# The Vector engine's order at the step boundary of a Runge-Kutta loop: a seed between two transposes, and FFN work ahead of the cubic term

## The chip, the cores and the metric

The kernel runs on one NeuronCore of a Trainium2 chip. The metric is the time of one execution on the device in microseconds (us). Engines are named as in the profile: PE (matmul), PEld (its weight load), DVE (Vector), ACT (Scalar), POOL (GpSimd), SP (the queue that issues most DMAs). L1313 is line 1313 of the kernel.

## The reference

```
x = x + attn(gru(cond, x))                    # 64 sequential GRU steps, then attention
x = x + ffn(rk4(cond, cond, drive=x))         # 64 sequential RK4 steps, FFN on their results

def _derivative(q, p, drive, coupling, bias):
    i_couple = jnp.tanh(q) @ coupling.T
    dq = q - q ** 3 / 3.0 - p + drive + i_couple + bias
    dp = EPSILON * (q + ALPHA - BETA * p)

dq1, dp1 = _derivative(q, p, drive, coupling, bias)
dq2, dp2 = _derivative(q + 0.5 * DT * dq1, p + 0.5 * DT * dp1, drive, coupling, bias)
dq3, dp3 = _derivative(q + 0.5 * DT * dq2, p + 0.5 * DT * dp2, drive, coupling, bias)
dq4, dp4 = _derivative(q + DT * dq3, p + DT * dp3, drive, coupling, bias)
q_next = clip(q + DT / 6.0 * (dq1 + 2 * dq2 + 2 * dq3 + dq4), -CLAMP, CLAMP)
```

The state q is 32 x 512. Four derivatives, each with a tanh and a product with a 512 x 512 matrix, follow one another in each of 64 steps. The FFN (gate, up, down, with its operands rounded to fp8) has 2048 rows, four steps' worth making a tile of 128 rows.

## The kernel before, in words

The program has three parts: the GRU, the attention, and from about 1009 us on the Runge-Kutta steps with the FFN woven in. Only the third is touched.

**Stages.** A step has four stages (st 0 to 3), stage number n = 4t + st. Four steps form a group g of 16 stages, counted k = 0 to 15. After each stage comes a "slot", a piece of the FFN for tiles made from earlier groups. The order on each engine is written out by hand: DVE, ACT, PE and POOL each run `stage` and `slot` in turn. Groups 0 to 2 and 15 are written out; groups 3 to 14 are a hardware loop of twelve passes. Groups 0 and most of 1 have no FFN work yet.

**One stage.** DVE turns the state in two halves (L1271, `state_turned`), ACT takes the tanh of each half (L961), PE multiplies with the coupling matrix in 32 matmuls (L750) into a PSUM bank that already holds a "seed", and DVE combines the bank with a cubic term `ebuf` (L1313). Then the next stage's halves are turned. The seed is written by DVE: for st 1 to 3 at L1292, right after the cubic term of the stage before; for st 0 at L1290, at the boundary between two steps. PE's L750 of a stage waits for its seed (rk_seed) and for the tanh of its first half, and from its 17th matmul on for the second half. After the 32 matmuls PE runs `mix_into` (L740), which waits for the seed of the next stage and has 1, 2 or 3 products in the stages 0, 1 and 2, and then the PE part of the slot (gate/up products L764, down products L811, transposes L775 and L785).

**The cubic term.** ACT squares the state into PSUM (L953), DVE makes `ebuf` from it (L1304). In st 1 to 3 ACT squares before the tanhs. In st 0 it squares after them, and it needs the clamped state, which DVE writes at L1326 (the boundary's last instruction), so L1304 of st 0 waits for a chain DVE, ACT, DVE.

**The boundary.** At the end of st 3 DVE runs: combination (L1313), both transposes (L1271), the seed of the next step (L1290, which waits for POOL's clamped p, rk_p, L519, and for the drive's sum), the clamp (L1326). Then st 0: cubic term (L1304), seed of st 1 (L1292), the slot's FFN piece, the drive's sum for the following step (L1281), combination (L1313).

**The FFN pieces that stand in st 0.** k = 0 and k = 12: one gate part (L1436, reads PSUM). k = 4: one gated part (L1444, reads PSUM, waits for POOL's L524 of slot 3). k = 8: a copy of one column (L1353) and `t_bits` on 768 columns (L1410, memory to memory), while POOL adds and subtracts the rounding grid of another tile (L538 and L543, 512 columns each, memory to memory).

Of the kernel before, what the change touches and what calls it, by code (L numbers as in the profile page):

```python
# [87 lines left out]
def wait_if(eng, sem, value):  # L88

    if not isinstance(value, int) or value > 0:  # L90
        eng.wait_ge(sem, value)
# [45 lines left out]
def gru_attn_rk4_ffn(nc, xT, x, cond_quad, cond_T, W_ih, W_hh, gate_bias, state_bias, gamma, Wq, Wkv, Wo,  # L137
                     couplingT, bias_quad, w_gate, w_up, w_down, down_idx, ident, mean_of, trig, mask,
                     x1_scr, q_scr, wgu_scr, wd_scr, scale_scr, tok_scr, out):
    with ExitStack() as ctx:  # L140
# [6 lines left out]
        def f32(a, *dims):  # L147
            n = 1
            for d in dims:
                n *= d  # L150
            v = mem[:, a:a + n]
            if len(dims) == 2:
                v = v.rearrange("p (a b) -> p a b", a=dims[0])
            if len(dims) == 3:
                v = v.rearrange("p (a b c) -> p a b c", a=dims[0], b=dims[1])
            return v
# [85 lines left out]
        qsT = f32(w.take(P), NC, B)  # L242
# [784 lines left out]
        def _(dve):  # L1027
# [237 lines left out]
            dve.tensor_scalar(pn[1], pn[1], -ALPHA / BETA, None, ALU.add).then_inc(rk_start, 1)  # L1265
            dve.wait_ge(rk_bits, 1)

            def state_turned(src):

                for half in range(2):  # L1270
                    dve.transpose(qsT[:, 2 * half:2 * half + 2, :].rearrange("p c b -> p (c b)"), src[:, half * 64:half * 64 + 64]).then_inc(rk_qT, 1)  # L1271
            state_turned(qn[3])
            dve.wait_ge(rk_start, 3)

            def driven(s):
                return ps[:, 4, (s % 2) * P:(s % 2 + 1) * P]

            def drive_sum(t, s, loads):

                dve.wait_ge(drive_ld[s], 16 * loads)  # L1280
                dve.tensor_tensor(driven(s), drive[s], bias_ps, ALU.add).then_inc(rk_drive, 1)  # L1281

            def seed(t, s, st):

                p = pn[(s - 1) % 2]
                o = ps[:, st % 2, 0:P]
                if st == 0:
                    dve.wait_ge(rk_drive, t + 1)
                    wait_if(dve, rk_p, t)
                    dve.tensor_tensor(o, driven(s), p, ALU.subtract).then_inc(rk_seed, 1)  # L1290
                else:
                    dve.scalar_tensor_tensor(out=o, in0=p, scalar=float(SEEDS[st][0]), in1=driven(s), op0=ALU.mult, op1=ALU.add).then_inc(rk_seed, 1)  # L1292
# [4 lines left out]
            def stage(g, s, st, last, fill):  # L1297
                t = 4 * g + s
                n = 4 * t + st
                qs = qn[(s - 1) % 4] if st == 0 else qst[st - 1]  # L1300
                stt = dve.scalar_tensor_tensor
                end = last and s == 3
                dve.wait_ge(rk_sq, n + 1)
                stt(out=ebuf, in0=ps[:, 5, 0:P], scalar=KEPT[st], in1=qs, op0=ALU.subtract, op1=ALU.mult).then_inc(rk_e, 1)  # L1304
                if st < 3:
                    seed(t, s, st + 1)
                fill()
                if st == 0 and not (last and s == 3):
                    drive_sum(t + 1, (s + 1) % 4, g + 1 + (s == 3))
                dve.wait_ge(rk_e, n + 1)  # L1310
                dve.wait_ge(rk_mm, n + 1)
                dst = qst[st] if st < 3 else ps[:, 4, 2 * P:3 * P]
                stt(out=dst, in0=ps[:, st % 2, 0:P], scalar=STEP[st], in1=ebuf, op0=ALU.mult,  # L1313
                    op1=ALU.subtract).then_inc(rk_qs if st < 3 else rk_pre, 1)
                if st < 3:
                    dve.wait_ge(rk_qs, n + 1)
                else:
                    dve.wait_ge(rk_pre, t + 1)
                if not (end and st == 3):
                    state_turned(dst)  # L1320
                if st == 3:
                    if not end:
                        seed(t + 1, (s + 1) % 4, 0)

                    wait_if(dve, q_wr[s], PRIMED + 16 * g)
                    dve.tensor_scalar(qn[s], dst, CLAMP, -CLAMP, ALU.min, ALU.max).then_inc(rk_qs, 1)  # L1326

# [121 lines left out]
            def group(g, rk, tile):  # L1449
                if not isinstance(g, int):  # L1450
                    base = counts["lead"] + (g - LEAD) * GROUP_STEPS
                else:
                    base = counts.get("next", 0)
                v = Steps(dve, rk_v, base)
                if isinstance(g, int) and g == 1:
                    dve.wait_ge(ffn_ld, 16 * 6)
                for k in range(16):
                    if rk:
                        stage(g, k // 4, k % 4, isinstance(g, int) and g == NTILE - 1, lambda: slot(v, k, tile, rk))
                    else:  # L1460
                        slot(v, k, tile, rk)
                if isinstance(g, int):
                    counts["next"] = counts.get("next", 0) + v.n
                    if g == LEAD - 1:
                        counts["lead"] = counts["next"]
                else:
                    assert v.n == GROUP_STEPS, v.n
                    counts["next"] += (NTILE - 1 - LEAD) * GROUP_STEPS
# [74 lines left out]
```

## Time and profile before

| | us |
|---|---|
| median of 3 runs | 1643.82 |
| lowest, highest | 1642.74, 1644.45 |
| the profiled execution | 1640.76 |
| its span, first to last instruction | 1638.8 |
| outside the span | 2.0 |
| third part, first combination to last | 1012.2 to 1593.0 |
| PE, DVE, ACT, POOL busy over the span | 91%, 68%, 36%, 23% |

Start times are in us from the span's start. The end of a DVE or ACT instruction is its start plus its length, but the next one can start before that: two records of one engine overlap, and the distance between starts is what an instruction costs in a row of them. Where the idle time before an instruction is given, the engine or line behind the arrow is what ended it.

### The profile page before, as it was taken

Reading aid. Unit: us, or ns where it says so; the run is one execution under the profiler, and the core shown is the slowest. Engines: PE = TensorE matmul, PEld = TensorE weight load, DVE = VectorE, ACT = ScalarE, POOL = GpSimd, SP = SyncE. Lnnn points to the kernel's source line nnn. Section 1 sums busy time; section 2 is a strip of 40 time slices with the busy share of each in tenths; the row PEclk is TensorE's granted clock in tenths of the full one; section 3 lists DMA queues with packets and bytes.
Section 4 is the critical chain, followed back from the end, with each engine's and each line's share of the span. In section 5 each row is a group of like instructions: output and inputs, shape, how many; then the busy total and the mean of one; then the engine's idle time right before and its main releaser. Section 6 shows DMA issues by size and latency. Waiting matters only on the chain.

```text
span 1638.8 us, 46339 instructions
## 1 busy us (share of the span) xinstructions
PE 1489.4 (91%) x16583; PEld 927.8 (57%) x16624; DVE 1119.8 (68%) x3565; ACT 588.7 (36%) x1903; POOL 381.5 (23%) x545
## 2 busy tenths in 40 slices
PE   5999999996799999999999997678899999999984
PEld 1333333334575767667675844556666666666662
DVE  1667667765774747575664732578888888888886
ACT  1444444441102020201102021455555555555552
POOL 0221221210000000000000000245655555556550
PEclk8999999997899999999999998999999999999996
DMA  7111112116101000100000024001111111111111
GB/s 304 44 45 50 51 46 65 51 47 167 9 1 26 0 26 0 26 0 26 6 19 13 13 64 163 21 25 29 40 40 40 33 35 32 35 32 43 37 38 33
DMA packets 91035, 72.79 MB, mean 44 GB/s; under 512 B 32480, under 2 KB 82912, under 8 KB 89824
## 3 DMA queue, kind: packets, MB, share of 16 engines
q1 hardware_dynamic: 71184, 59.35, 12.4%
q10 hardware_dynamic: 18032, 6.88, 1.7%
q0 software_dynamic: 1760, 5.77, 1.2%
q8 instruction: 37, 0.61, 0.2%
q14 instruction: 22, 0.18, 0.0%
HBM read 55.03 MB, written 16.94 MB: 44 GB/s over the span
## 4 chain that ended last, share of the span: by engine, by line
PE 73%; DVE 13%; ACT 5%; issue 5%; DMA 1%; POOL 1%; DVEq 0%; SPq 0%; POOLq 0%; ACTq 0%
PE ps L655 13%; PE ps L645 13%; PE ps L750 11%; PE ps L583 11%; PE ps L595 10%; PE ps L689 3%; PE ps L713 3%; ACT mem L961 3%; DVE mem L1313 2%; DVE mem L1271 2%; PE ps L740 2%; ACT ps L953 2%; PE ps L764 1%; PE ps L666 1%; DVE ps L1281 1%
## 5 line engine op out<-in xcount | busy, mean ns | idle before, releaser
L750 PE MATMUL ps<-mem 128*32 128x128 f32 x8192 | 278.8, 276 | 68.5 <-ACT mem L961 65.8
L750 PEld LDWEIGHTS ps<-mem 128*32 128x32 f32 x8192 | 211.4, 110 | 143.0 <-ACT mem L961 97.2
L645 PE MATMUL ps<-mem 128*128 128x512 f32 x512 | 224.6, 592 | 0.0
L655 PE MATMUL ps<-mem 128*128 128x256 f32 x1024 | 222.3, 379 | 0.0
L655 PEld LDWEIGHTS ps<-mem 128*128 128x128 f32 x1024 | 194.0, 190 | 26.0
L509 POOL TENSOR_TENSOR mem<-mem 128x128 f32<-128x128 f32 x64 | 30.8, 481 | 732.8 <-ACT mem L956 732.8
L583 PE MATMUL ps<-mem 128*32 128x384 f32 x2048 | 181.6, 497 | 10.2 <-DMA mem<-in_W_ih 6.3
L595 PE MATMUL ps<-mem 128*32 128x384 f32 x2048 | 177.6, 488 | 2.4 <-DVE mem L1098 2.4
L928 ACT ACTIVATE mem<-mem 128x512 f32<-128x512 f32 x32 | 19.7, 630 | 391.0 <-DVE mem L1211 391.0
L645 PEld LDWEIGHTS ps<-mem 128*128 128x128 f32 x512 | 95.6, 190 | 109.7 <-issue 109.3
L961 ACT ACTIVATE mem<-mem 128x64 f32<-128x64 f32 x512 | 102.9, 248 | 116.5 <-DVE mem L1271 116.4
L953 ACT ACTIVATE ps<-mem 128x128 f32<-128x128 f32 x256 | 72.0, 281 | 182.2 <-DVE mem L1313 175.8
L740 PE MATMUL ps<-mem 128*128 128x128 f32 x768 | 137.0, 301 | 0.0
L513 POOL TENSOR_TENSOR mem<-mem 128x128 f32<-128x128 f32 x192 | 99.8, 520 | 155.7 <-ACT mem L956 149.6
L595 PEld LDWEIGHTS ps<-mem 128*32 128x32 f32 x2048 | 62.9, 110 | 109.5 <-issue 81.0
L583 PEld LDWEIGHTS ps<-mem 128*32 128x32 f32 x2048 | 64.3, 111 | 105.5 <-issue 90.8
L740 PEld LDWEIGHTS ps<-mem 128*128 128x128 f32 x768 | 100.2, 190 | 38.4 <-issue 25.9
L1174 DVE TENSOR_TENSOR mem<-ps,mem 64x256 f32<-64x256 f32 x272 | 114.7, 422 | 8.5
L1172 DVE TENSOR_TENSOR mem<-ps,mem 128x256 f32<-128x256 f32 x136 | 57.8, 425 | 69.9 <-PE ps L666 40.8
L764 PE MATMUL ps<-mem 128*128 128x352 bf16 x512 | 100.3, 322 | 3.5 <-DVE mem L1436 3.4
L480 POOL COPY mem<-mem 128x128 f32 (+1 forms) x64 | 37.7, 590 | 276.2 <-DVE mem L1098 276.2
L1304 DVE SCALAR_TENSOR_TENSOR mem<-ps,mem 128x128 f32<-128x128 f32 x256 | 74.5, 291 | 22.4 <-ACT ps L953 22.4
(139 smaller groups left out, 2097.0 us busy)
## 6 DMA issues: line engine op xcount, KB each, us to landing
mem<-x_scr SPq DMA_DIRECT2D x128, 64.0 KB, 1.8
mem<-in_xT SPq DMA_DIRECT2D x64, 64.0 KB, 1.9
mem<-in_Wq SPq DMA_DIRECT2D x1, 4096.0 KB, 12.4
mem<-in_Wo SPq DMA_DIRECT2D x1, 4096.0 KB, 20.7
mem<-in_x SPq DMA_DIRECT2D x16, 256.0 KB, 2.8
x_scr<-mem SPq DMA_DIRECT2D x32, 128.0 KB, 2.3
q_scr<-mem SPq DMA_DIRECT2D x64, 64.0 KB, 1.6
mem<-q_scr SPq DMA_DIRECT2D x64, 64.0 KB, 1.9
```

The lines of the kernel that those rows point to most:

```text
L513: tt(pacc, pacc, pw[1 + st], ALU.add).then_inc(rk_pa, 1)
L583: mm = pe.matmul(ps[32 * j:32 * j + 32, par, 0:3 * P].rearrange("p (g n) -> p g n", g=3), xt[par][:, c, :], wih[:, c, :].rearrange("p (g j ...
L595: mm = pe.matmul(ps[32 * j:32 * j + 32, par, P:4 * P].rearrange("p (g n) -> p g n", g=3), hT[1 - par][:, c, :], whh[:, c, :].rearrange("p ...
L645: mm = pe.matmul(ps[:, 6 + pr, :], aoT[:, h, pr * P:pr * P + P], wo[:, h, :], start=(h == 0), stop=(h == HEADS - 1))
L655: mm = pe.matmul(ps[:, h % Q_BANKS, 0:BLK], wq[:, c, h * DH:(h + 1) * DH], xnb[:, c, :], start=(c == 0), stop=(c == NC - 1))
L740: pe.matmul(ps[:, st % 2, 0:P], mix[m], (None, qn[(s - 1) % 4], *qst)[k], start=False, stop=False, skip_group_check=True)
L750: mm = pe.matmul(ps[32 * j:32 * j + 32, st % 2, 0:P], thT[:, c, :], ct[:, c, j * P:(j + 1) * P], start=False, stop=(c == NC - 1), skip_gro ...
L764: mm = pe.matmul(ps[:, 2 + order % 2, 0:GU_N], qxT[:, c, :], (wgT if gate else wuT)[:, c, m * GU_N:(m + 1) * GU_N], start=(c == 0), stop=( ...
L953: act.activation(ps[:, 5, 0:P], src, ACT.Square, scale=(STEP[st] / 3) ** 0.5).then_inc(rk_sq, 1)
L961: act.activation(thT[:, 2 * half:2 * half + 2, :], qsT[:, 2 * half:2 * half + 2, :], ACT.Tanh).then_inc(rk_th, 1)
L1174: dve.tensor_tensor(share[b:b + DH // 2], src[a:a + DH // 2], bcast(trigs[:, tr + 1, :], BLK_B)[a:a + DH // 2], ALU.mult).then_inc(done, 1)
L1304: stt(out=ebuf, in0=ps[:, 5, 0:P], scalar=KEPT[st], in1=qs, op0=ALU.subtract, op1=ALU.mult).then_inc(rk_e, 1)
```

## The change

`state_turned` is split so that each half can be written alone. At the boundary the next step's seed goes between the two transposes. In stage 0 the FFN's piece (`fill`) goes ahead of the cubic term, and the drive's sum stands behind the seed of stage 1. Stages 1 to 3 keep their order.

```diff
+            def turned_half(src, half):
+
+                dve.transpose(qsT[:, 2 * half:2 * half + 2, :].rearrange("p c b -> p (c b)"), src[:, half * 64:half * 64 + 64]).then_inc(rk_qT, 1)
+
...
                 end = last and s == 3
+                if st == 0:
+                    fill()
                 dve.wait_ge(rk_sq, n + 1)
                 stt(out=ebuf, in0=ps[:, 5, 0:P], scalar=KEPT[st], in1=qs, op0=ALU.subtract, op1=ALU.mult).then_inc(rk_e, 1)
                 if st < 3:
                     seed(t, s, st + 1)
-                fill()
-                if st == 0 and not (last and s == 3):
+                if st:
+                    fill()
+                elif not end:
                     drive_sum(t + 1, (s + 1) % 4, g + 1 + (s == 3))
...
-                if not (end and st == 3):
+                if st < 3:
                     state_turned(dst)
-                if st == 3:
+                else:
                     if not end:
+                        turned_half(dst, 0)
                         seed(t + 1, (s + 1) % 4, 0)
-
+                        turned_half(dst, 1)
                     wait_if(dve, q_wr[s], PRIMED + 16 * g)
                     dve.tensor_scalar(qn[s], dst, CLAMP, -CLAMP, ALU.min, ALU.max).then_inc(rk_qs, 1)
```

Only DVE's row changes; the rows of PE, ACT, POOL and SP stay in their order. DVE in the loop, from the boundary into k = 4, before (L1271 the transposes, L1290 the seed of st 0, L1326 the clamp, L1304 the cubic term, L1292 the seed of st 1, L1444 the FFN piece, L1281 the drive's sum, L1313 the combination):

```order
L1271 STREAM_TRANSPOSE mem<-ps 128x64 [waits rk_pre]
L1271 STREAM_TRANSPOSE mem<-ps 128x64
L1288 REGISTER_ALU
L1290 TENSOR_TENSOR ps<-ps,mem 128x128 [waits rk_p,rk_drive]
L91 ISA
L1326 TENSOR_SCALAR mem<-ps 128x128 [waits q_wr0]
L1303 ISA
L1304 SCALAR_TENSOR_TENSOR mem<-ps,mem 128x128 [waits rk_sq]
L1292 SCALAR_TENSOR_TENSOR ps<-mem,ps 128x128
L1444 SCALAR_TENSOR_TENSOR mem<-ps,mem 128x352 [waits f_sgu,f_u]
L1281 TENSOR_TENSOR ps<-mem,ps 128x128 [waits drive_ld2]
L1313 SCALAR_TENSOR_TENSOR mem<-ps,mem 128x128 [waits rk_mm,rk_e]
```

The same place now (the lines are, in that order of names: L1270, L1293, L1333, L1309, L1295, L1451, L1284, L1319):

```order
L1270 STREAM_TRANSPOSE mem<-ps 128x64 [waits rk_pre]
L1291 REGISTER_ALU
L1293 TENSOR_TENSOR ps<-ps,mem 128x128 [waits rk_p,rk_drive]
L1270 STREAM_TRANSPOSE mem<-ps 128x64
L91 ISA
L1333 TENSOR_SCALAR mem<-ps 128x128 [waits q_wr0]
L1451 SCALAR_TENSOR_TENSOR mem<-ps,mem 128x352 [waits f_sgu,f_u]
L1308 ISA
L1309 SCALAR_TENSOR_TENSOR mem<-ps,mem 128x128 [waits rk_sq]
L1295 SCALAR_TENSOR_TENSOR ps<-mem,ps 128x128
L1284 TENSOR_TENSOR ps<-mem,ps 128x128 [waits drive_ld2]
L1319 SCALAR_TENSOR_TENSOR mem<-ps,mem 128x128 [waits rk_mm,rk_e]
```

The seed has changed places with the second transpose, and the FFN piece, with its waits on POOL (f_sgu) and PE (f_u), has moved past the cubic term and the seed of st 1. DVE in the loop, from the boundary into k = 8, before (L1353 the copy of a column, L1410 `t_bits`):

```order
L1290 TENSOR_TENSOR ps<-ps,mem 128x128 [waits rk_p,rk_drive]
L1326 TENSOR_SCALAR mem<-ps 128x128 [waits q_wr1]
L1303 ISA
L1304 SCALAR_TENSOR_TENSOR mem<-ps,mem 128x128 [waits rk_sq]
L1292 SCALAR_TENSOR_TENSOR ps<-mem,ps 128x128
L1353 COPY mem<-mem 128x1 [waits f_gated]
L1409 ISA
L1410 TENSOR_SCALAR mem<-mem 128x768 [waits f_vt]
L1281 TENSOR_TENSOR ps<-mem,ps 128x128 [waits drive_ld3]
```

And now (L1360 the copy, L1417 `t_bits`):

```order
L1293 TENSOR_TENSOR ps<-ps,mem 128x128 [waits rk_p,rk_drive]
L1270 STREAM_TRANSPOSE mem<-ps 128x64
L1333 TENSOR_SCALAR mem<-ps 128x128 [waits q_wr1]
L1360 COPY mem<-mem 128x1 [waits f_gated]
L1416 ISA
L1417 TENSOR_SCALAR mem<-mem 128x768 [waits f_vt]
L1308 ISA
L1309 SCALAR_TENSOR_TENSOR mem<-ps,mem 128x128 [waits rk_sq]
L1295 SCALAR_TENSOR_TENSOR ps<-mem,ps 128x128
L1284 TENSOR_TENSOR ps<-mem,ps 128x128 [waits drive_ld3]
```

Here the piece that moved is a memory-to-memory instruction. PE's row at this place, unchanged, after the 32 matmuls of k = 8:

```order
L738 REGISTER_ALU
L740 MATMUL ps<-mem 128x128 [waits rk_seed]
L811 MATMUL ps<-mem 128x512 [waits f_tTcp]
L811 MATMUL ps<-mem 128x512 x2
L748 ISA [waits rk_seed]
L750 MATMUL ps<-mem 32x128 [waits rk_th]
```

The down products and the next stage's L750 are queued behind L740, which waits for the seed of st 1.

## Rows read from the trace of the kernel before

**Rows 1.** The page: busy time by engine; the chain that ended last.

```profile
PE 1489.4 (91%) x16583; PEld 927.8 (57%) x16624; DVE 1119.8 (68%) x3565; ACT 588.7 (36%) x1903; POOL 381.5 (23%) x545
PE 73%; DVE 13%; ACT 5%; issue 5%; DMA 1%; POOL 1%; DVEq 0%; SPq 0%; POOLq 0%; ACTq 0%
```

**Rows 2.** Timeline, DVE, k = 15 into k = 0: start, length, engine, line, operation.

```profile
1301.46 0.30 DVE L1313 SCALAR_TENSOR_TENSOR ps<-ps,mem 128x128 f32<-128x128 f32 x1 [0.47 <-PE ps L750]
1301.79 0.38 DVE L1271 STREAM_TRANSPOSE mem<-ps 128x64 f32<-128x64 f32 x2
1302.10 0.27 DVE L1290 TENSOR_TENSOR ps<-ps,mem 128x128 f32<-128x128 f32 x1
1302.27 0.27 DVE L1326 TENSOR_SCALAR mem<-ps 128x128 f32<-128x128 f32 x1
1302.90 0.29 DVE L1304 SCALAR_TENSOR_TENSOR mem<-ps,mem 128x128 f32<-128x128 f32 x1 [0.35 <-ACT ps L953]
1303.10 0.28 DVE L1292 SCALAR_TENSOR_TENSOR ps<-mem,ps 128x128 f32<-128x128 f32 x1
1303.30 0.58 DVE L1436 SCALAR_TENSOR_TENSOR mem<-ps,mem 128x352 f32<-128x352 f32 x1
1303.79 0.28 DVE L1281 TENSOR_TENSOR ps<-mem,ps 128x128 f32<-128x128 f32 x1
1303.99 0.28 DVE L1313 SCALAR_TENSOR_TENSOR mem<-ps,mem 128x128 f32<-128x128 f32 x1
```

**Rows 3.** Timeline, ACT, the same boundary and the next stage.

```profile
1302.08 0.40 ACT L961 ACTIVATE mem<-mem 128x64 f32<-128x64 f32 x2 [1.54 <-DVE mem L1271]
...
1304.58 0.40 ACT L961 ACTIVATE mem<-mem 128x64 f32<-128x64 f32 x2
```

**Rows 4.** Timeline, PE: k = 15, 0 and 1; last, k = 9.

```profile
1300.24 1.08 PE L750 MATMUL ps<-mem 128*32 128x128 f32 x32 [0.18 <-ACT mem L961]
...
1302.50 1.08 PE L750 MATMUL ps<-mem 128*32 128x128 f32 x32
1303.51 0.49 PE L740 MATMUL ps<-mem 128*128 128x128 f32 x2
...
1304.89 1.08 PE L750 MATMUL ps<-mem 128*32 128x128 f32 x32 [0.30 <-ACT mem L961]
...
1323.04 1.08 PE L750 MATMUL ps<-mem 128*32 128x128 f32 x32 [0.29 <-ACT mem L961]
```

**Rows 5.** Timeline, ACT and PE, first boundary of group 0, written out, no FFN.

```profile
1020.24 0.40 ACT L961 ACTIVATE mem<-mem 128x64 f32<-128x64 f32 x2 [1.62 <-DVE mem L1271]
...
1020.64 1.08 PE L750 MATMUL ps<-mem 128*32 128x128 f32 x32 [1.15 <-ACT mem L961]
```

**Rows 6.** Timeline, POOL and DVE, k = 3 and 4, the same loop pass.

```profile
1310.78 0.93 POOL L524 TENSOR_TENSOR mem<-mem 128x352 f32<-128x352 f32 x1
...
1313.02 0.28 DVE L1313 SCALAR_TENSOR_TENSOR mem<-ps,mem 128x128 f32<-128x128 f32 x1
```

**Rows 7.** Timeline, POOL, then DVE, boundary into k = 8, the same loop pass.

```profile
1320.07 1.27 POOL L538 TENSOR_TENSOR mem<-mem 128x512 f32<-128x512 f32 x1
1321.50 1.65 POOL L543 TENSOR_TENSOR mem<-mem 128x512 bf16<-128x512 f32 x1 [0.16 <-POOL mem L538]
...
1320.39 0.27 DVE L1326 TENSOR_SCALAR mem<-ps 128x128 f32<-128x128 f32 x1
...
1321.47 0.55 DVE L1410 TENSOR_SCALAR mem<-mem 128x768 uint32<-128x768 uint32 x1
...
1322.13 0.28 DVE L1313 SCALAR_TENSOR_TENSOR mem<-ps,mem 128x128 f32<-128x128 f32 x1
```

**Rows 8.** Timeline, POOL, then DVE, boundary into k = 8 of group 2, written out.

```profile
1102.29 1.27 POOL L543 TENSOR_TENSOR mem<-mem 128x512 bf16<-128x512 f32 x1
...
1102.71 1.27 DVE L1410 TENSOR_SCALAR mem<-mem 128x768 uint32<-128x768 uint32 x1
...
1104.10 0.28 DVE L1313 SCALAR_TENSOR_TENSOR mem<-ps,mem 128x128 f32<-128x128 f32 x1
```

More of the change, by code:

```diff
@@ L1266, in _ @@
             dve.wait_ge(rk_bits, 1)
+            def turned_half(src, half):
+                dve.transpose(qsT[:, 2 * half:2 * half + 2, :].rearrange("p c b -> p (c b)"), src[:, half * 64:half * 64 + 64]).then_inc(rk_qT, 1)
             def state_turned(src):
-                for half in range(2):
-                    dve.transpose(qsT[:, 2 * half:2 * half + 2, :].rearrange("p c b -> p (c b)"), src[:, half * 64:half * 64 + 64]).then_inc(rk_qT, 1)
+                turned_half(src, 0)
+                turned_half(src, 1)
             state_turned(qn[3])
```

## The prediction

> **What bounds the kernel now.** I read the page first: PE is busy 91% and holds 73% of the chain that ended last [rows 1], which would say that nothing on DVE matters. That is a mean over three parts. The change sits in the third, so I went to the timelines of DVE, ACT, PE and POOL at the boundaries between steps. In the loop the four boundaries are alike in every one of twelve passes, and each is met here once: into k = 0, 4, 8 and 12.
>
> Into k = 0 the reader is to see three things [rows 2]. After the clamp at 1302.27 DVE idles 0.35 until ACT's square is there. Then everything starts in a row, 0.20 apart, with the FFN piece taking 0.49 (1303.30 to 1303.79). The combination at 1303.99 shows no idle: it waited for DVE's own row. PE had its product earlier: in the stage before, the combination came 1.22 after the start of L750 (1300.24 to 1301.46) [rows 2, 4], so with L750 at 1302.50 it could have run at 1303.72. And PE's L750 of k = 1 waits 0.30 for ACT [rows 4], so the 0.27 reach PE. In stage 0, DVE's order is the bound; about 0.3 us later it is PE.
>
> **The seed between the transposes.** ACT's first tanh starts at 1302.08, and PE follows at 1302.50, 0.42 later; one stage on the lag is 0.31 (1304.58 to 1304.89) [rows 3, 4]. The extra 0.11 is the seed: it ends at 1302.37, 0.13 before L750. The two transposes stand 0.15 apart or so, the next instruction 0.16 behind the second (1301.79 and 0.38 for two, then 1302.10) [rows 2]. The seed now starts near 1301.95, ends at 1302.22, and the first tanh becomes the bound: L750 at 1302.39, 0.11 sooner. The second transpose ends 0.17 later, its tanh near 1302.65; PE needs it from the 17th matmul, 0.54 after 1302.39, that is 1302.93. Nothing is late. The clamp keeps its place, so the square and the cubic term do too. In the written-out groups the lag is 0.40 even in stages whose seed is long there, and also at the boundary (1020.24 to 1020.64) [rows 5]: there I take no gain, and so none for the eight boundaries without FFN. Bounds: 0 to 0.11 each, eight times.
>
> **The FFN piece ahead, into k = 0 and 12.** The gate part reads a product that PE finished before the boundary. It starts about 0.19 after the clamp, 1302.46, and costs 0.49: the cubic term starts at 1302.95 instead of 1302.90. The seed of st 1 follows at 1303.15, the drive's sum at 1303.35, and the combination could run at 1303.55; PE's product allows 1302.39 + 1.22 = 1303.61. That is 0.38 sooner than 1303.99. But PE has a second condition, L740, which waits for the seed of st 1 and has the FFN product and L750 of k = 1 behind it. L740 stood at 1303.51, 0.41 behind that seed, though PE itself was only just free (1.01 after L750), so the true lag is somewhere from 0.35 (the seed's length 0.28 and the 0.06 which a tanh's end is ahead of L750) to 0.41. Now L740 starts at 1303.50 to 1303.56. The 0.30 of idle before L750 of k = 1 bound what is left: PE's work ends it at 1304.59, or 1304.52 with the usual overlap of two records. So L750 starts 0.25 to 0.37 sooner; I take **0.33** for each, since most of the terms favour the later half. What comes after is tied to L750 and shifts with it. The branch at the loop's end is before the piece of k = 0; the 0.35 idle hid it, and it may cost up to 0.1 there.
>
> **Into k = 4.** This boundary lies 9.03 later (1313.02 against 1303.99) [rows 2, 6]. DVE would begin the gated part at 1311.49, but it needs POOL's L524, which ends at 1311.71 [rows 6]. With a lag of 0.08 it starts at 1311.79, the cubic term at 1312.28, the seed of st 1 at 1312.48, and L740 at 1312.83 to 1312.89, against 1312.54 before (1303.51 + 9.03). L750 of k = 5, which stood at 1313.92 (1304.89 + 9.03), can then start at 1313.84 to 1313.97. The wait that vanished on ACT returns as one on POOL: **0.02** gained, bounds -0.05 to 0.08; if POOL's end is in truth earlier than its rough span says, up to 0.33.
>
> **Into k = 8, the loop.** Here the piece is L1410, memory to memory, and POOL's L538 and L543 run at the same time. In group 2 L1410 starts at 1102.71 with L543 under way until 1103.56, lasts 1.27 instead of 0.55, and ends 0.42 after L543 [rows 7, 8]: it waited for the whole of it. In the loop it slips into the gap between L538 (ends 1321.34) and L543, and now L543 takes 1.65 instead of 1.27 [rows 7]. So one holds the other out. Moved up, L1410 is asked for at 1320.39 + 0.19 + 0.06 = 1320.64, in the middle of L538. It ends at 1321.34 + 0.42 = 1321.76, and the cubic term starts at 1321.68 (the next record starts some 0.08 before the end, as behind the gate part in rows 2), the seed of st 1 at 1321.89, L740 at 1322.24 to 1322.30. Before, by the distance to rows 2 (18.11), L740 stood at 1321.62; behind it are the down products and L750 of k = 9, which stood at 1323.04 with 0.29 idle [rows 4]. The 0.62 to 0.68 of delay use up that idle time, 0.29 to 0.36 with the overlap, and the rest is lost: 0.26 to 0.39, I take **-0.31**. The combination itself moves from 1322.13 to 1322.29. This is the step where the move harms the loop.
>
> **The same place written out** (groups 2 and 15). There L1410 was already held up by L543. Asked for during L538, which is over by the start of L543 at 1102.29, it ends at 1102.71 at the latest, the cubic term starts at 1102.63 and the combination 0.60 later at 1103.23, against 1104.10 [rows 8]: 0.87 or a little more. I take 0.9 for both groups.
>
> The Trainium skill bears on who gets in first. SBUF — State Buffer, § Who interferes with whom, says that DVE in a two-port mode and GpSimd share a pair of ports, held for the whole instruction by whoever issues first. By that, L1410, issued during L538, gets the pair ahead of L543, which is issued after L538 has ended, and the sum stays as worked out; were it the other way the slow case below would hold. The trace agrees on the whole-instruction hold (0.42 after L543's end, in rows 8); a case with both waiting is not in it.
>
> **The sum.** One loop pass: 0.33 + 0.02 - 0.31 + 0.33 = 0.37, times 12 is 4.4. Written out: four boundaries into k = 0 or 12 (group 1, two in group 2, one in group 15) at 0.28, the difference of 1303.99 and 1303.72 without a seed's gain, 1.1; two into k = 4 at 0.2, since there PE starts 0.1 later anyway and has slack, 0.4; two into k = 8, 1.8; the last one, without a drive's sum, 0.1. Together 3.4. All: 7.8 us. Against the profiled execution: 1640.76 - 7.8 = 1633.0, of which 2.0 lie outside the span. That execution was 3.1 under the median of the runs; against the median: 1643.82 - 7.8 = **1636.0**.
>
> **Rivals.** 1. *No hold at k = 8.* If L1410 passed beside L538, k = 8 would gain 0.28 like the others: 12 x (0.33 + 0.02 + 0.28 + 0.33) = 11.5, and 14.9 with the rest, 1628.9; with POOL's L524 early too, 12 x 0.31 more, 1625.2. For it: POOL's spans are rough. Against: L543's 1.65 and L1410's 1.27 can hardly both be rough ends [rows 7, 8].
> 2. *POOL keeps the port: slower.* If L543 goes straight behind L538, L1410 waits until 1322.77 + 0.42 = 1323.19 in the loop, the seed of st 1 comes at 1323.32, L740 at 1323.67 and L750 of k = 9 at 1324.73, 1.69 late. A pass: 0.68 - 1.69 = -1.01, times 12 is -12.1; written out the two places lose 0.4 each instead of gaining 1.8, leaving 0.8. Net 11.3 slower, 1655.1. It decides by who is first after 1321.34. Against it: the loop leaves 0.16 between POOL's two instructions [rows 7], and L1410 already entered in it.
> 3. *Faint.* The lags at L740 all lie at their far ends (0.25, -0.05, -0.39, 0.25 less 0.1 for the branch): a pass gives about 0, and 3.4 stay; with the seed's wait on POOL's clamped p (rk_p) holding up the second transpose and the clamp by 0.05 to 0.1 here and there, 1641.0 to 1643.
> 4. *Order not as written.* DVE's row was compared and has moved as said; no chance is kept for this.
>
> **Chances.** Forecast (1632.5 to 1639.8) 0.60; rival 1 0.14; rival 2 0.10; rival 3 0.14; anything else 0.02. The range from 1628 to 1641 takes in the forecast and most of rival 1, and leaves out rival 2 and most of 3. A measurement of this kernel can tell about 0.2%, 3.3 us, from no change. Faster by more (under 1640.5): 0.60 + 0.14 + 0.03 = 0.77; the same 0.12; slower 0.11.
>
> **What would show it.** L750 0.31 behind the first tanh at the loop's boundaries; the cubic term of k = 0 0.68 after the clamp with no idle before it; the gated part of k = 4 released by POOL L524; L1417 at k = 8 about 1.1 long and ending 0.42 after L538; the combination-to-combination time into k = 0 and 12 at 2.15 to 2.2 instead of 2.53 (1301.46 to 1303.99 in rows 2). A loop pass shorter by 0.3 to 0.5 confirms the sum, by 0.9 or more rival 1, longer by 1.0 rival 2. The forecast is wrong if L1417 is short, or if L543 comes before it.

## The result and the profile after

| | before | after |
|---|---|---|
| median, us | 1643.28 | 1631.74 |
| lowest, highest | 1640.08, 1644.45 | 1631.14, 1632.17 |
| ratio to before | | 0.9943, 95% interval 0.9927 to 0.9959 |
| the profiled execution | 1640.76 | 1631.14 |
| its span | 1638.8 | 1629.2 |

The change makes the kernel faster by 0.6% by this ratio; the two medians lie 11.5 us (0.7%) apart. The prediction was 1636.0 with a range of 1628 to 1641.

The timelines of the changed kernel at the boundary into k = 0 answer to [rows 2 to 4]. Columns: start, length, engine, line, operation, idle time before it and what ended it. DVE, then ACT and PE:

```profile
1296.88 0.30 DVE L1319 SCALAR_TENSOR_TENSOR ps<-ps,mem 128x128 f32<-128x128 f32 x1 [0.47 <-PE ps L750]
1297.21 0.25 DVE L1270 STREAM_TRANSPOSE mem<-ps 128x64 f32<-128x64 f32 x1
1297.38 0.29 DVE L1293 TENSOR_TENSOR ps<-ps,mem 128x128 f32<-128x128 f32 x1
1297.59 0.24 DVE L1270 STREAM_TRANSPOSE mem<-ps 128x64 f32<-128x64 f32 x1
1297.75 0.25 DVE L1333 TENSOR_SCALAR mem<-ps 128x128 f32<-128x128 f32 x1
1298.05 0.58 DVE L1443 SCALAR_TENSOR_TENSOR mem<-ps,mem 128x352 f32<-128x352 f32 x1
1298.56 0.28 DVE L1309 SCALAR_TENSOR_TENSOR mem<-ps,mem 128x128 f32<-128x128 f32 x1
1298.75 0.28 DVE L1295 SCALAR_TENSOR_TENSOR ps<-mem,ps 128x128 f32<-128x128 f32 x1
1298.95 0.29 DVE L1284 TENSOR_TENSOR ps<-mem,ps 128x128 f32<-128x128 f32 x1
1299.14 0.28 DVE L1319 SCALAR_TENSOR_TENSOR mem<-ps,mem 128x128 f32<-128x128 f32 x1
...
1297.49 0.62 ACT L961 ACTIVATE mem<-mem 128x64 f32<-128x64 f32 x2 [1.54 <-DVE mem L1270]
...
1297.81 1.08 PE L750 MATMUL ps<-mem 128*32 128x128 f32 x32
1299.09 0.49 PE L740 MATMUL ps<-mem 128*128 128x128 f32 x2 [0.21 <-DVE ps L1295]
```

The idle 0.35 of DVE ahead of the cubic term is gone. L750 starts 0.32 behind the first tanh and 0.93 behind the boundary's combination (1.04 before). L740, which came 1.01 behind L750, now comes 1.28 behind it and was idle for 0.21 until the seed of st 1 (L1295). That seed now holds PE's next L750. The combination itself (L1319 at 1299.14) stands 0.19 behind the drive's sum without idle time and 1.33 behind L750, where PE's product would allow 1.22: at k = 0 it is still late by DVE's own row, by about 0.1.

Into k = 4, POOL and then DVE:

```profile
1305.99 0.93 POOL L524 TENSOR_TENSOR mem<-mem 128x352 f32<-128x352 f32 x1
...
1306.58 0.25 DVE L1333 TENSOR_SCALAR mem<-ps 128x128 f32<-128x128 f32 x1
1306.76 0.56 DVE L1451 SCALAR_TENSOR_TENSOR mem<-ps,mem 128x352 f32<-128x352 f32 x1
```

The gated part starts at 1306.76, while POOL's L524 runs until 1306.92. It doesn't wait for it.

Into k = 12, POOL, DVE and PE:

```profile
1324.01 0.29 POOL L519 TENSOR_SCALAR mem<-mem 128x128 f32<-128x128 f32 x1 [0.22 <-POOL mem L513]
...
1324.41 0.30 DVE L1293 TENSOR_TENSOR ps<-ps,mem 128x128 f32<-128x128 f32 x1
...
1324.85 1.08 PE L750 MATMUL ps<-mem 128*32 128x128 f32 x32 [0.46 <-DVE ps L1293]
```

POOL's clamped p (L519) ends at 1324.30, the seed starts 0.11 later, and L750 waits for the seed: it comes 1.03 behind the boundary's combination (1323.82), almost as late as the 1.04 of before.

Into k = 8, POOL, DVE and PE, answering to [rows 7]:

```profile
1314.94 1.28 POOL L538 TENSOR_TENSOR mem<-mem 128x512 f32<-128x512 f32 x1
1316.38 1.39 POOL L543 TENSOR_TENSOR mem<-mem 128x512 bf16<-128x512 f32 x1 [0.16 <-POOL mem L538]
...
1315.57 1.07 DVE L1417 TENSOR_SCALAR mem<-mem 128x768 uint32<-128x768 uint32 x1
1316.56 0.28 DVE L1309 SCALAR_TENSOR_TENSOR mem<-ps,mem 128x128 f32<-128x128 f32 x1
...
1317.10 0.49 PE L740 MATMUL ps<-mem 128*128 128x128 f32 x2 [0.61 <-DVE ps L1295]
```

L1417 lasts 1.07 and ends at 1316.64, 0.42 after L538 (1316.22), as L1410 had ended 0.42 after L543 in [rows 8]. It was first in line, and L543, which started at 1316.38, was held instead.

The steps, from combination to combination (a step begins at the boundary named; mean of like passes):

| us | before | after | gained | forecast |
|---|---|---|---|---|
| step from k = 0 | 9.03 | 8.83 | 0.20 | 0.33 |
| from k = 4 | 9.08 | 8.73 | 0.35 | 0.02 |
| from k = 8 | 9.12 | 9.37 | -0.25 | -0.31 |
| from k = 12 | 9.03 | 8.78 | 0.25 | 0.33 |
| a loop pass | 36.27 | 35.72 | 0.55 | 0.37 |
| twelve passes | 435.4 | 428.5 | 6.9 | 4.4 |
| group 2 and group 15 | 37.5, 37.7 | 35.8, 35.9 | 3.5 | 3.1 |

With 0.3 in group 1 that is 10.7 us. The spans differ by 9.6. The execution profiled after had three stages in the groups 0 and 1 that lasted 2.92, 2.53 and 3.06 instead of 2.2, which makes 1.9 us together. The view of windows shows the granted clock there (columns: window, length, busy time of PE, PEld, DVE, ACT, POOL with counts, clock, DMA share, GB/s): 0.72 and 0.74 as the means of two windows of 6 us, against 1.00 later on. In single microseconds of the first window, from 1031 to 1033, it goes down to 0.50, the lower level of 1.2 GHz, just behind 0.71 us in which PE had idled ahead of an L750:

```profile
1028.00:1034.00 6.00, 5.29 (x91) 4.31 (x95) 2.94 (x14) 2.56 (x12) 1.36 (x3) 0.72 0.09 25
1058.00:1064.00 6.00, 5.73 (x106) 4.74 (x100) 2.85 (x11) 1.97 (x10) 1.82 (x4) 0.74 0.01 1
1290.00:1330.00 40.00, 37.36 (x700) 26.54 (x696) 35.52 (x131) 23.36 (x89) 24.22 (x35) 1.00 0.16 44
```

The profile before has 1.00 in the same two windows and no such stage there. Experiments 3 and 4 have the changed kernel's code in the groups 0 and 1; there these groups took 71.9 us in one and 70.0 in the other, first combination to last, and 71.9 in the changed kernel. So the slow stages are not the change's. Without them 0.8 us of the difference remain, and they lie outside this stretch. The experiments are therefore judged by the length of a loop pass, which within a profile repeats within 0.03 from the second pass on (experiment 2 apart), and by the time of the whole beside it.

### The profile page after: what moved, and what is told of

Same layout as the page of the kernel before. It is cut to its first block, busy times and chain, and to the rows that moved or that the text cites. A ratio compares the mean times of both kernels' runs of the same rounds, so it can differ in the third digit from the quotient of the medians.

```text
span 1629.2 us, 46380 instructions
## 1 busy us (share of the span) xinstructions
PE 1495.9 (92%) x16624; PEld 929.1 (57%) x16624; DVE 1127.0 (69%) x3565; ACT 590.6 (36%) x1903; POOL 378.4 (23%) x545
## 4 chain that ended last, share of the span: by engine, by line
PE 77%; DVE 12%; issue 4%; ACT 4%; POOL 2%; DMA 1%; DVEq 0%; POOLq 0%; SPq 0%; ACTq 0%
PE ps L655 14%; PE ps L645 14%; PE ps L750 11%; PE ps L583 11%; PE ps L595 10%; PE ps L740 4%; PE ps L689 3%; PE ps L713 3%; PE ps L764 3%; ACT mem L961 2%; DVE mem L1319 2%; DVE mem L1270 1%; PE ps L811 1%; POOL mem L513 1%; PE ps L666 1%
## 5 line engine op out<-in xcount | busy, mean ns | idle before, releaser
L750 PE MATMUL ps<-mem 128*32 128x128 f32 x8192 | 280.6, 278 | 45.5 <-ACT mem L961 36.7
L750 PEld LDWEIGHTS ps<-mem 128*32 128x32 f32 x8192 | 212.9, 110 | 116.7 <-ACT mem L961 76.0
L961 ACT ACTIVATE mem<-mem 128x64 f32<-128x64 f32 x512 | 109.9, 250 | 123.9 <-DVE mem L1270 118.6
L740 PE MATMUL ps<-mem 128*128 128x128 f32 x768 | 138.0, 303 | 11.2 <-DVE ps L1295 9.8
L740 PEld LDWEIGHTS ps<-mem 128*128 128x128 f32 x768 | 101.0, 191 | 53.7 <-DVE ps L1295 27.4
L956 ACT ACTIVATE mem<-mem 128x128 f32<-128x128 f32 x320 | 87.8, 293 | 0.0
```

The source lines that it names most:

```text
L740: pe.matmul(ps[:, st % 2, 0:P], mix[m], (None, qn[(s - 1) % 4], *qst)[k], start=False, stop=False, skip_group_check=True)
L750: mm = pe.matmul(ps[32 * j:32 * j + 32, st % 2, 0:P], thT[:, c, :], ct[:, c, j * P:(j + 1) * P], start=False, stop=(c == NC - 1), skip_gro ...
L956: act.activation(pw[of], (pn[(s - 1) % 2], src)[of > 0], ACT.Copy, scale=float(weight)).then_inc(rk_w, 1)
L961: act.activation(thT[:, 2 * half:2 * half + 2, :], qsT[:, 2 * half:2 * half + 2, :], ACT.Tanh).then_inc(rk_th, 1)
```

## Experiments

All are edits of the changed kernel, against the kernel before on the same chip (medians 1643.12 for the first four, 1644.12 for the last three).

**1. Only the FFN piece ahead.**

```diff
                         turned_half(dst, 0)
-                        seed(t + 1, (s + 1) % 4, 0)
                         turned_half(dst, 1)
+                        seed(t + 1, (s + 1) % 4, 0)
```

> Only the FFN piece is moved ahead; the seed stands behind both transposes again, as before the change. Theory (the clamp is what counts now: the changed kernel's clamp comes 0.87 to 0.96 after the combination at the boundary instead of 0.81, the cubic term, the seed of st 1 and PE's L740 follow from it, and the seed between the transposes earns nothing once L740 decides): in the loop the boundaries into k = 0, 4 and 12 get 0.06 to 0.12 shorter, k = 8 stays, since POOL's L538 decides there; a pass of about 35.5 instead of 35.72, 2 to 3 us faster than the changed kernel, 1629. Rival (the seed's 0.11 of earlier L750 is worth its place at each boundary): a pass of 36.05, 4 us slower than the changed kernel, 1636.

Measured 1631.96, ratio 0.9943 (0.9921 to 0.9965); a pass of 35.77. Neither came: the seed's place is worth 0.05 a pass, 0.6 us in all. By boundary, the step got 0.09 longer from k = 4, 0.03 shorter from k = 0, and changed by 0.02 or less from k = 8 and 12. DVE and PE at k = 4 of this kernel show why my theory was half right:

```profile
1271.01 0.27 DVE L1333 TENSOR_SCALAR mem<-ps 128x128 f32<-128x128 f32 x1
1271.21 0.56 DVE L1451 SCALAR_TENSOR_TENSOR mem<-ps,mem 128x352 f32<-128x352 f32 x1
...
1272.09 0.29 DVE L1284 TENSOR_TENSOR ps<-mem,ps 128x128 f32<-128x128 f32 x1
1272.46 0.29 DVE L1319 SCALAR_TENSOR_TENSOR mem<-ps,mem 128x128 f32<-128x128 f32 x1
...
1271.24 1.08 PE L750 MATMUL ps<-mem 128*32 128x128 f32 x32 [0.20 <-ACT mem L961]
1272.25 0.49 PE L740 MATMUL ps<-mem 128*128 128x128 f32 x2
```

L740 is back at 1.01 behind L750, as expected, but now L750 itself is 0.1 later and the combination waits for PE: 1.22 behind L750, and 0.17 after DVE could have started it. The earlier clamp and the earlier seed nearly cancel: each relieves one of two conditions that lie about 0.1 us apart.

**2. Only the seed between the transposes.**

```diff
-                if st == 0:
-                    fill()
...
-                if st:
-                    fill()
-                elif not end:
+                fill()
+                if st == 0 and not end:
```

> Only the seed is moved between the transposes; the FFN piece stands behind the cubic term again. Theory (DVE's row decides stage 0 here, so the later clamp costs 0.06 or more per filled boundary; and into k = 8 L1410 was asked for 0.03 before POOL's L543 in the kernel before, so 0.06 later it finds L543 in front and waits for all of it): into k = 0, 4 and 12 2.6 instead of 2.53, into k = 8 3.7 instead of 2.56, a loop pass of about 37.6, 16 us slower than before, 1659. Rival 1 (L1410 still gets in): a pass of 36.5, 3 us slower than before, 1646. Rival 2 (the seed between is worth 0.11 each): 5 us faster than before, 1638.

Measured 1657.22, ratio 1.0076 (1.0053 to 1.01). Nine passes of twelve took 37.64 to 37.79, as the theory had it, with 3.74 or 3.75 into k = 8. Three took 36.54 or 36.55, as in rival 1, with 2.63. Into k = 0, 4 and 12 it was 2.57, 2.57 and 2.66, where 2.6 was expected. Without the FFN piece moved ahead, the change of the seed alone costs 14 us. The two kinds of pass, POOL and DVE in each; first one of the three, then one of the nine:

```profile
1181.40 1.70 POOL L543 TENSOR_TENSOR mem<-mem 128x512 bf16<-128x512 f32 x1 [0.16 <-POOL mem L538]
1181.42 0.55 DVE L1414 TENSOR_SCALAR mem<-mem 128x768 uint32<-128x768 uint32 x1
...
1217.94 1.26 POOL L543 TENSOR_TENSOR mem<-mem 128x512 bf16<-128x512 f32 x1 [0.16 <-POOL mem L538]
1217.97 1.66 DVE L1414 TENSOR_SCALAR mem<-mem 128x768 uint32<-128x768 uint32 x1
```

The starts lie 0.02 to 0.03 apart in both, and POOL's record has the earlier one even where DVE got in, so the records don't tell who asked first; whoever gets in runs its natural time, and the other waits for the whole of it, 1.1 longer for DVE, 0.4 for POOL. In the kernel before, L1410's record started 0.03 to 0.04 ahead of L543's in every pass [rows 7], and DVE got in each time: its place there had been won by 0.03 us.

**3. The order of before at k = 8 in the loop.**

```diff
+                late = st == 0 and s == 2 and not isinstance(g, int)
-                if st == 0:
+                if st == 0 and not late:
                     fill()
...
-                if st:
+                if st or late:
                     fill()
-                elif not end:
+                if st == 0 and not end:
...
                         turned_half(dst, 0)
+                        if s == 1 and not isinstance(g, int):
+                            turned_half(dst, 1)
                         seed(t + 1, (s + 1) % 4, 0)
-                        turned_half(dst, 1)
+                        if not (s == 1 and not isinstance(g, int)):
+                            turned_half(dst, 1)
```

> The changed kernel, but the boundary into k = 8 in the loop's twelve passes keeps the order of before (both transposes, seed, clamp, cubic term, seed of st 1, FFN piece, drive's sum). Theory (the 0.25 that a pass loses at k = 8 is L1417 waiting for all of POOL's L538): combination to combination into k = 8 back at 2.56, L543 back at 1.65, a pass of about 35.47, 3 us faster than the changed kernel, 1628.7. Rival (the loss at k = 8 is the later clamp and the order as such, or it comes back elsewhere): within 1 us of the changed kernel.

Measured 1628.99, ratio 0.9913 (0.9896 to 0.9929); a pass of 35.49, 2.57 into k = 8. These are the theory's numbers. The edit restores the whole order at k = 8, so it shows what that boundary loses (0.23 a pass), and not yet that POOL's hold is the reason; that is for experiment 5. POOL and DVE there:

```profile
1281.91 1.64 POOL L543 TENSOR_TENSOR mem<-mem 128x512 bf16<-128x512 f32 x1 [0.16 <-POOL mem L538]
...
1281.88 0.55 DVE L1421 TENSOR_SCALAR mem<-mem 128x768 uint32<-128x768 uint32 x1
```

**4. The wait that the prediction read into k = 4.**

```diff
-                dve.wait_ge(f_sgu, GU_T * i + m + 1)
+                dve.wait_ge(f_sgu, GU_T * i + m + 1 + (m == 2))
```

> The changed kernel, and the gated part of k = 4 waits for POOL's L524 of slot 3, as the prediction took it to do, instead of the one of slot 1. Theory (the changed kernel does not wait there, so the wait is new): L1451 of k = 4 starts 0.2 to 0.27 later, the step from k = 4 is 0.24 longer, a pass of 35.96, 3 us slower than the changed kernel, 1634.6. Rival (it waited already, and POOL's span is rough): no difference.

Measured 1634.78, ratio 0.9949 (0.9926 to 0.9973); a pass of 36.03, the combination into k = 4 after 2.43 instead of 2.15, the step 0.31 longer (0.24 was expected). POOL, DVE and PE:

```profile
1269.27 0.93 POOL L524 TENSOR_TENSOR mem<-mem 128x352 f32<-128x352 f32 x1
...
1270.32 0.58 DVE L1451 SCALAR_TENSOR_TENSOR mem<-ps,mem 128x352 f32<-128x352 f32 x1 [0.21 <-POOL mem L524]
...
1271.35 0.49 PE L740 MATMUL ps<-mem 128*128 128x128 f32 x2 [0.35 <-DVE ps L1295]
```

With the wait put in, DVE idles 0.21 for POOL and starts 0.12 after L524 ends, and the step loses almost all that it gained: 0.35 - 0.31 = 0.04, where the prediction had 0.02. The mechanism was priced rightly, for a wait that the kernel doesn't have.

**5. POOL's two grid instructions on 32 columns.**

```diff
-                        pool.tensor_tensor(vq, vq, eq, ALU.add).then_inc(f_xa, 1)
+                        pool.tensor_tensor(vq[:, 0:32], vq[:, 0:32], eq[:, 0:32], ALU.add).then_inc(f_xa, 1)
...
-                        pool.tensor_tensor(qx8, vq, eq, ALU.subtract).then_inc(f_q8, 1)
+                        pool.tensor_tensor(qx8[:, 0:32], vq[:, 0:32], eq[:, 0:32], ALU.subtract).then_inc(f_q8, 1)
...
+            dve.memset(qx8, 0.0)
```

This kernel leaves out the rounding of the other 480 columns, so it serves only to read a time.

> The changed kernel with POOL's two grid instructions of the slots 7 and 8 (L538, L543) on 32 of 512 columns; the rest of the operand is zero, so the FFN's first rounding is left out for most columns. Theory (at k = 8 L1417 is held by L538 alone): L1417 lasts 0.55 instead of 1.07, the combination into k = 8 comes after 2.2 instead of 2.71 and the next after 2.15 instead of 2.22, a pass of 35.1 instead of 35.72, 7 us faster than the changed kernel, 1624. Rival (L1417 is slow there for its own reasons, ACT writing the other half of the same rows among them): still 1.07, a pass of 35.7.

Measured 1625.41, ratio 0.9891 (0.9872 to 0.9911); a pass of 35.20, 2.18 into k = 8 and 2.23 for the next stage (2.15 was expected there). L1418, the same instruction, is back at its natural time:

```profile
1278.00 0.26 POOL L543 TENSOR_TENSOR mem<-mem 128x32 bf16<-128x32 f32 x1 [0.16 <-POOL mem L538]
...
1278.22 0.55 DVE L1418 TENSOR_SCALAR mem<-mem 128x768 uint32<-128x768 uint32 x1
```

The rival is out. POOL's two instructions at full length cost the changed kernel 0.52 a pass, about 6 us. The edit shortens both; that it is L538 that holds DVE is read from the changed kernel's trace, where L1417 is already waiting before L543 starts.

**6. The seed of st 1 right behind the clamp, with the order of before at k = 8.** Experiment 3's kernel and

```diff
+                if st == 0:
+                    seed(t, s, 1)
...
-                if st < 3:
+                if 0 < st < 3:
                     seed(t, s, st + 1)
```

> The changed kernel with the boundary into k = 8 as before in the loop, and, in every stage 0, the seed of st 1 right behind the clamp, ahead of FFN piece and cubic term, since it needs only p and the drive's sum. Theory (PE's L740 waits for that seed and holds the FFN product and L750 of the next stage): L740 goes back to 1.01 behind L750; k = 0, 4, 12 come 0.18, 0.04 and 0.05 sooner at the next L750; at k = 8 L1423 is asked for 0.2 earlier, ahead of POOL's L543 by more, waits 0.07 for L538 and the step gets 0.25 shorter. A pass of 34.95 to 35.05, 12 x 0.5 = 6 us faster than the same without it (1629.0), 1623. Rival (L740's wait is hidden, DVE's row and the tanhs decide): within 1.5 us of 1629.

Measured 1624.21, ratio 0.9893 (0.9871 to 0.9915); a pass of 35.07 against 35.49 in experiment 3. At k = 4, DVE, then PE:

```profile
1268.95 0.28 DVE L1295 SCALAR_TENSOR_TENSOR ps<-mem,ps 128x128 f32<-128x128 f32 x1
1269.14 0.57 DVE L1457 SCALAR_TENSOR_TENSOR mem<-ps,mem 128x352 f32<-128x352 f32 x1
1269.63 0.27 DVE L1312 SCALAR_TENSOR_TENSOR mem<-ps,mem 128x128 f32<-128x128 f32 x1
...
1268.84 1.08 PE L750 MATMUL ps<-mem 128*32 128x128 f32 x32
1269.85 0.49 PE L740 MATMUL ps<-mem 128*128 128x128 f32 x2
```

L740 is 1.01 behind L750 again with the seed long there. The steps from k = 0 (8.67 against 8.84) and from k = 8 (8.93 against 9.13) carry nearly all of it.

**7. The seed of st 1 right behind the clamp, nothing else.** The same move on the changed kernel.

> The changed kernel with nothing else than the seed of st 1 right behind the clamp in every stage 0. Theory (as above): at k = 0, 4 and 12 0.18, 0.04 and 0.05; at k = 8 L1423 still waits for all of L538, but the cubic term's and PE's rows behind it are one instruction shorter, 0.2 to 0.29; a pass of 35.15 to 35.25, 6 us faster than the changed kernel, 1625.5. Rival: within 1.5 us of the changed kernel, 1631.7.

Measured 1625.14, ratio 0.9902 (0.9877 to 0.9927); a pass of 35.21 against 35.72. In both experiments the pass came within 0.02 of the theory's span, and the rival is out: the late seed costs the changed kernel 0.5 a pass. But PE's wait is less than half of that. At k = 8, DVE, then PE:

```profile
1277.93 0.28 DVE L1295 SCALAR_TENSOR_TENSOR ps<-mem,ps 128x128 f32<-128x128 f32 x1
1278.18 0.87 DVE L1418 TENSOR_SCALAR mem<-mem 128x768 uint32<-128x768 uint32 x1
...
1279.37 0.28 DVE L1320 SCALAR_TENSOR_TENSOR mem<-ps,mem 128x128 f32<-128x128 f32 x1
...
1278.83 0.49 PE L740 MATMUL ps<-mem 128*128 128x128 f32 x2
1280.27 1.08 PE L750 MATMUL ps<-mem 128*32 128x128 f32 x32 [0.30 <-ACT mem L961]
```

The seed is written in time that DVE would spend held by L538 (L1418 lasts 0.87 instead of 1.07), and the combination comes after 2.51 instead of 2.71; L740 follows L750 without idle time, and the next L750 waits for ACT again. Into k = 0 the combination comes after 2.17 instead of 2.27: between clamp and FFN piece the seed adds 0.10, not the 0.20 that it costs in a row. These two make 0.30 of the 0.51 that a pass gains, and they are time of DVE's row; the other 0.2 is what PE's L740 had cost behind the combination.

The fastest kernel of the study is that of experiment 6, 1.1% under the kernel before and 0.5% under the changed one by the two ratios (0.9893 and 0.9943). Experiments 1 to 4 and 5 to 7 were timed in two sets, so 1628.99 is compared with 1624.21 only by the pass. The intervals of experiments 6 and 7 overlap, and it is their passes (35.07 and 35.21) that tell them apart.

## Why the prediction was right or wrong

**What bounds stage 0.** Right for the kernel before: the combination was late by DVE's row. With the FFN piece ahead it falls back to what PE allows at k = 4 (2.15: L750 at 0.94 and 1.22 more) and at k = 12 (2.24: L750 at 1.03 and 1.21 more). At k = 0 it does not: 2.27, which is 0.12 behind what PE allows, and DVE's row still decides. The prediction's sign of 2.15 to 2.2 for k = 0 and 12 did not come.

**The seed between the transposes.** L750 came 0.11 sooner at k = 0 and 4, as worked out, 0.08 at k = 8, and 0.01 at k = 12, where its seed waits for POOL's clamped p. There was no gain in the written-out groups without FFN (2.22 a stage as before), as assumed. "The clamp keeps its place" was wrong: it comes 0.87 behind the combination at k = 0 and 4 and 0.96 at k = 12, not 0.81. A seed between two transposes costs 0.17 ahead of it and 0.21 behind it where the row before took 0.16 and 0.17, and at k = 12 it starts at 0.59 instead of 0.50 because POOL's clamped p ends only at 0.48, and the second transpose is held with it. The latter stood among the mishaps of rival 3.

**The piece ahead, into k = 0 and 12.** 0.20 and 0.25 instead of 0.33. L740 behind the seed of st 1 was named as the second condition, and its lag is 0.34 (1307.44 to 1307.78), at the near end of my bounds. What was under-sized is the stretch from combination to cubic term: 1.49 was worked out, 1.68 measured at k = 0 and 1.62 at k = 12, from the later clamp and, at k = 0, from 0.30 between clamp and FFN piece where k = 4 has 0.18. The idle 0.35 had hidden the loop's turn (its branch and register work): at the eleven boundaries where one pass follows another 0.30 to 0.35 lie between clamp and FFN piece, and 0.17 or 0.18 into group 2, into the first pass and into group 15, where there is none. The prediction allowed up to 0.1 for it and did not put it in the sum.

**Into k = 4.** Wrong, and the largest miss: 0.35 instead of 0.02, 4 us in twelve passes. The failing step is "it needs POOL's L524, which ends at 1311.71". The gated part of k = 4 is part 2, and `gate_scaled` of part 2 stands in POOL's slot 1; slot 3 holds part 3, which is needed at k = 5. The words ahead of the prediction ("waits for POOL's L524 of slot 3") have the same mistake. The semaphore's name was right and its count wasn't. Experiment 4 shows that the price of such a wait was read rightly.

**Into k = 8.** Right in mechanism and size: L1417 asked for during L538 ends 0.42 after it (1.07 long), L543 is held behind it, the cubic term starts 0.08 before L1417's end, and the step loses 0.25 (bounds 0.26 to 0.39, again with L740's lag at the near end). Experiments 3 and 5 put it on POOL's two instructions, and the trace on L538. Written out, 0.96 and 0.97 were gained at these places where 0.9 was taken.

**The sum.** Terms of 0.33, 0.02, -0.31 and 0.33 became 0.20, 0.35, -0.25 and 0.25. Errors of both signs left a pass 0.18 short of the truth, and the loop's first pass gave a further 0.35: 10.7 us against 7.8. The prediction took all twelve passes for alike, but before the change the first one had 2.70 into k = 0 instead of 2.53, and after it 2.15 instead of 2.27. The 0.28 for the written-out boundaries is 0.27 by its own two figures, which changes nothing. The measured median is inside the range by luck in part: 1631.74 lies under the band of the forecast (1632.5 to 1639.8), in the part that was there for rival 1, a pass was 0.55 shorter where 0.3 to 0.5 was to confirm the sum, and without the partial cancelling the sum would have missed by more.

**The rivals.** Rival 1 (no hold at k = 8) would have shown a pass shorter by 0.9 or more; its price was nearly that of experiment 5 (35.20, 1.07 shorter than before). Rival 2 (POOL first) did not happen in the changed kernel in any pass, and it did in nine of twelve passes of experiment 2, at a price of 1.1: real and near, though tied to another order than the one where I had put it. Rival 3 (the lags at their far ends) did not come, apart from the held transpose at k = 12.

## What to carry to other kernels

When a row of instructions has two late conditions (here DVE's row for the combination, and one seed for PE's next product), moving work ahead of one of them uncovers the other: write an instruction that depends on nothing recent ahead of everything that waits, as experiment 7 does for another 0.5 us a pass, about 6 us. Before moving a memory-to-memory instruction of DVE, look at what POOL does in the very same tenth of a microsecond, at the old place and the new one. And where a wait is on a counted semaphore, work out which producer's turn makes the count before pricing it; the line that increments it is not enough.

## What the runs showed of the hardware

- Two engines whose starts lie within 0.02 to 0.03 us of each other are served in either order: in experiment 2 POOL got in first in nine passes and DVE in three, with the same code and a pass of 37.65 or 36.54. The kernel before had this tie at 0.03 us and DVE first in all twelve.
- The hold is for the whole instruction in both directions: L1417 1.07 instead of 0.55 behind L538, L1414 1.66 behind L543, L543 1.64 to 1.70 instead of 1.27 behind DVE. A DVE instruction that was held ends 0.42 after the other one, 0.13 less than its own 0.55.
- The Trainium skill, SBUF — State Buffer, § Who interferes with whom, has the port pair go to whoever issues first. With DVE waiting since 1315.57 and POOL's next instruction from 1316.38 on, all twelve passes of the changed kernel agree: L1417 ends 0.42 behind L538 in each, and L543 takes 1.38 or 1.39 behind it instead of 1.27.
- The loop's turn costs a busy engine time and an idle one nothing: on DVE 0.12 us or more in the changed kernel (0.30 to 0.35 between clamp and FFN piece, 0.17 or 0.18 without it), while before the change it lay in 0.35 of idle time.
